# A decoder, cross attention and mixture-of-experts kernel: the cross attention written anew, with all groups in one written-out order over several groups in flight

## What is computed

```
x = layernorm(x + decoder(x))            # 4 layers of causal attention and MLP, and a final norm
x = layernorm(x + xattn(x, ctx_768))
x = layernorm(x + experts(x))            # 8 experts, top 2 of them weighted

def xattn(x, y):                         # y: 120 context rows per sequence
    q = (x @ Wq + bq).reshape(B, N, 16, 16); k, v = likewise from y
    attn = softmax(einsum('bnhd,bmhd->bhnm', q, k) / sqrt(16))
    out  = einsum('bhnm,bmhd->bnhd', attn, v).reshape(B, N, 256)
    return relu(out @ W1 + b1) @ W2 + b2
```

## Time and profile before

| | us |
|---|---|
| median of 3 runs (3950.48 to 3954.08) | 3953.2 |
| the profiled execution itself | 3950.34 |
| its span | 3948.5 |

### The profile page before, as it was taken

The page is one execution under the profiler, slowest core; times in us unless marked ns, Lnnn a source line. Parts: engine busy times, 40 slices in busy tenths (PEclk is TensorE's granted clock), DMA queues, the critical chain, the costliest instruction groups (busy, mean ns, idle before and its releaser), DMA issues. The chain is left out here.

```text
span 3948.5 us, 98572 instructions
## 1 busy us (share of the span) xinstructions
PE 3497.6 (89%) x37088; PEld 2401.6 (61%) x37088; DVE 2361.2 (60%) x4859; ACT 1892.8 (48%) x2713; POOL 1415.3 (36%) x1324
## 2 busy tenths in 40 slices
PE   5899999999999999999955667679999999999998
PEld 3566666666666676666633444446666666666666
DVE  5777777777767777777436676444444434434356
ACT  4666676666766667766623333332222322223222
POOL 1243233332333323333323222134444444444443
PEclk8999999999999999999977778789999999999999
DMA  3100111001110011100011111020000000000000
GB/s 110 45 24 29 45 33 45 27 26 45 33 45 27 26 45 33 45 27 26 18 49 38 44 37 33 23 113 11 11 22 0 22 0 22 20 2 11 0 12 32
DMA packets 103895, 124.22 MB, mean 31 GB/s; under 512 B 17664, under 2 KB 94208, under 8 KB 101120
## 3 DMA queue, kind: packets, MB, share of 16 engines
q1 hardware_dynamic: 103520, 118.78, 9.1%
HBM read 50.13 MB, written 8.39 MB: 15 GB/s over the span
## 5 line engine op out<-in xcount | busy, mean ns | idle before, releaser
L2088 POOL TENSOR_TENSOR e_hT<-e_h,e_hT 128x512 f16<-128x512 f32 x512 | 591.1, 1156 | 775.4 <-DVE e_hT L2054 775.4
L75 PE MATMUL bank<-e_half,e_hT 128*128 128x256 f16 x6144 | 713.7, 273 | 2.6 <-POOL e_hT L2088 2.5
L991 DVE TENSOR_REDUCE mx<-maxima_pair 128x4 f16<-128x1024 f32 (+1 forms) x384 | 470.2, 1224 | 376.8 <-PE maxima_pair L482 374.9
L75 PEld LDWEIGHTS bank<-e_half,e_hT 128*128 128x128 f16 x6144 | 601.8, 98 | 127.2 <-issue 3.3
L2054 DVE CAST e_hT<-e_h 128x512 f16<-128x512 f32 x512 | 301.2, 591 | 448.0 <-ACT e_h L2012 447.8
L75 PE MATMUL bank<-xT,w_half 128*128 128x512 f16 x2304 | 535.4, 383 | 29.4 <-ACT mrow L770 18.3
L1091 POOL TENSOR_TENSOR QK<-qk,QK 128x512 f16<-128x512 f32 x128 | 148.1, 1157 | 1026.3 <-ACT QK L721 985.9
L789 ACT ACTIVATE PR<-scores_pair 128x1024 f32<-128x1024 f32 x384 | 393.0, 1024 | 177.5 <-PE scores_pair L499 97.2
L2012 ACT ACTIVATE e_h<-scores_pair,e_b 128x512 f32<-128x512 f32 x256 | 175.9, 687 | 495.1 <-PE scores_pair L75 449.0
L1098 POOL TENSOR_TENSOR hT<-h,hT 128x512 f16<-128x512 f32 x256 | 291.9, 1168 | 296.8 <-ACT hT L776 296.8
L2012 ACT ACTIVATE e_h<-maxima_pair,e_b 128x512 f32<-128x512 f32 x256 | 175.7, 687 | 456.8 <-PE maxima_pair L75 445.1
(11 more groups left out here) (162 smaller groups left out, 5676.1 us busy)
## 6 DMA issues: line engine op xcount, KB each, us to landing
QS<-QK SPq DMA_DIRECT2D x240, 128.0 KB, 2.1
KS<-QK SPq DMA_DIRECT2D x192, 128.0 KB, 2.1
e_raw<-in_expert_weights SPq DMA_DIRECT2D x16, 1024.0 KB, 5.1
w_raw<-in_weights SPq DMA_DIRECT2D x48, 256.0 KB, 3.1
c_x<-in_x SPq DMA_DIRECT2D x8, 512.0 KB, 4.2
xT_halves<-c_xT SPq DMA_DIRECT2D x16, 256.0 KB, 2.6
out<-e_z SPq DMA_DIRECT2D x8, 512.0 KB, 2.9
x<-in_x SPq DMA_DIRECT2D x1, 3584.0 KB, 15.3
```

What stands on the lines that cost most here:

```text
L75: last = pe.matmul(out, stat(a, k), mov(b, k), start=(k == 0 and n == 0), stop=(k == tiles - 1 and n == 2))
L991: dve.tensor_reduce(out, src, AX.X, ALU.max, negate=True).then_inc(mx_in.sem, 1)
L2088: pool.tensor_tensor(low, h32[:, m % 2, :], hT[odd][0][:, m, :], ALU.subtract)\
```

## The change

`cross` no longer has loops or kinds of bodies. Every engine walks over `BODIES`, and in each body does, in a hand-set order, pieces of up to seven groups. What changes besides the order:

- One joint root for three norms: the first norm of group n, the sum's norm of group n-1 and the last norm of group n-5. Its steps are on 128x12, with twelve aggregations.
- ScalarE makes the high halves of Q, K and of the hidden tiles by a second activation from PSUM; VectorE's two kinds of casts are gone. `h32` has four parts instead of two.
- GpSimd takes over the addition of b2 (`add_bias`, 128x1024) and the low half of the context (`context_low`, 128x480).
- The last norm writes into x, and ScalarE's copy into x is gone. The context halves and the rows of VS for the values are doubled.
- The split of the weights comes ahead of the first sum's norm.

In the diff the first `hidden_high` is VectorE's, the new functions behind it are ScalarE's and GpSimd's, and the last part is the second half of VectorE's body.

```diff
+    BODIES = range(-4, NG + 3)
+    NORMS, LAG = 3, 5
...
-    norm_buf = [NormBuffers(sb, f"c_norm{i}", shared["dve_gate"]) for i in range(3)]
...
+        def joint_root(n):
+            for i, g in enumerate((n, n - 1, n - LAG)):
+                if has(g):
+                    dve.wait_ge(stats_in[i].sem, stats_in[i].after(g))
+                    part_from_wait(dve, shared["dve_gate"])
+            for t in range(NORMS * TT):
+                dve.bn_aggr(mean_var[:, t, :], stats[:, t, :]).then_inc(rooted.sem, 1)
...
-        def hidden_high(n):
-                dve.tensor_copy(hT[0][:, m, :], h32[:, m % 2, :]).then_inc(h_h.sem, 1)
+        def hidden_high(n, m):
+            act.wait_ge(H_ps.sem, H_ps.after(n, m + 1))
+            act.activation(hT[0][:, m, :], work("H", n, m)[:, :], ACT.Relu,
+                           bias=cols[:, 4 + m:5 + m], scale=1.0 / WS).then_inc(h_h.sem, 1)
...
+        def query_key_high(n, m):
+            query_key(n, m, QK[0], qk_h)
...
+        def add_bias(n):
+            pool.wait_ge(z1.sem, z1.after(n))
+            pool.tensor_tensor(x[:, bass.ds(n * TT, TT), :], z[1][:, :, :], row["b2"].unsqueeze(1)
+                               .to_broadcast([P, TT, D]), ALU.add).then_inc(z1b.sem, 1)
...
-        body(PRE, -1, True, False, False)
-        body(HEAD, 0, True, True, False)
-        with eng.Fori(1, NG - 1) as n:
-            body(STEADY, n, True, True, True)
+        for n in BODIES:
...
+            if has(n):
+                maxima(n, 3, 0)
+            if has(n - 2):
+                last_stats(n - 2)
+            if has(n + 2):
+                sum_stats(n + 2)
+            if has(n):
+                maxima(n, 3, 1)
+            if 0 <= n + 3 < NG + LAG:
+                joint_root(n + 3)
+            if has(n + 2):
+                sum_scaled(n + 2)
+            if has(n - 2):
+                last_scaled(n - 2)
+            if has(n + 1):
+                maxima(n + 1, 0, 0)
+            if has(n - 3):
+                router_weights(n - 3)
```

More of the change, by code:

```diff
@@ L1261, in cross, with work, free_tile @@
+    def work(stage, n, k):
+        return W[AT[stage, n, k] % R]
+    def free_tile(pe, stage, n, k):
+        before = AT[stage, n, k] - R
+        if before >= 0:
+            stage, of, part = TILES[before]
+            for signal, each in READERS[stage]:
+                pe.wait_ge(signal.sem, signal.after(of, (part + 1) * each))
+        return W[before % R]
     block_ctx = ExitStack()
@@ L1294, in halves @@
                 sp.wait_ge(s.sem, s.after(n))
-                part_from_wait(sp, shared["sp_gate"])
-                sp.dma_start(xT_halves[half, :, :, bass.ds(n * GT, GT)], xT[1][half][:, :, :])\
+                sp.dma_start(xT_halves[half, :, :, n * GT:(n + 1) * GT], xT[1][half][:, :, :])\
                   .then_inc(halves_out.sem, 16)
[L1299 to L1306, removed]
-            if ahead:
-                heads(n + 1, 1)
-            if back:
-                halves(n - 1)
         sp.dma_start(rows[:, :], dram["cross_rows"].partition_broadcast(P)).then_inc(s_const, 16)
@@ new lines, in outputs @@
+        def outputs(n, k):
+            bank = free_tile(pe, "Y", n, k)
+            if k == 0:
+                pe.wait_ge(h_h.sem, h_h.after(n))
+                pe.wait_ge(h_l.sem, h_l.after(n))
+            for u in range(2):
+                t = 2 * k + u
+                last = split_matmuls(pe, bank[:, u * D:(u + 1) * D], lambda h, kk: hT[h][:, kk, t * P:(t + 1) * P],
+                                     lambda h, kk: views["f2"][h][:, kk, :], KF2)
+            last.then_inc(Y_ps.sem, 1)
@@ L1554, in out_rows @@
             act.activation(OTs[:, c, :], O[:, :], ACT.Copy).then_inc(o_in.sem, 1)
-        def hidden(kind, n):
-            for m in range(KF2):
-                act.wait_ge(H_ps.sem, H_ps.after(n - 1, m + 1))
-                for s in (h_h, h_l):
-                    act.wait_ge(s.sem, s.after(n - 1, m - 1) if m >= 2 else s.after(n - 2, KF2 - 1 + m))
-                act.activation(h32[:, m % 2, :], work(kind, ("H", m))[:, :], ACT.Relu,
-                               bias=cols[:, 4 + m:5 + m], scale=1.0 / WS).then_inc(h_f.sem, 1)
@@ new lines, in scale_tiles, with first_stats, first_scaled @@
+        def scale_tiles(i, n, src, out, done):
+            rstd = root[NEWTON % 2]
+            dve.wait_ge(rooted.sem, rooted.after(n))
+            for t in range(TT):
+                at = i * TT + t
+                dve.tensor_scalar(out(t), src(t), mean_var[:, at, 0:1], rstd[:, at:at + 1], ALU.subtract, ALU.mult)\
+                   .then_inc(done.sem, 1)
+        def first_stats(n):
+            tile_stats(0, x_tiles(n))
+        def first_scaled(n):
+            dve.wait_ge(z1.sem, z1.after(n - 1))
+            scale_tiles(0, n, x_tiles(n), lambda t: z[0][:, t:t + 1, :], zf)
+            if n == 0:
+                split_weights()
```

881 lines of the change are left out of this document (483 added, 398 removed), and 4 rows, old and new, of the table ORDER.

## The result

The changed kernel takes 3772.76 us in the median of four runs, the kernel before 3952.86: a ratio of 0.9551 [0.9533, 0.957], 180 us less. I had predicted 3784, in a range from 3748 to 3832. The profiled execution took 3773.66 us, its span is 3771.8.

What follows compares the result with a forecast made beforehand. Engines taking turns in a chain were taken to bound the body; reordered, VectorE's 31 + 8 and 2 of waits make 41 us, eight bodies 292, with the ends 169 us saved: 3784, range 3748 to 3832.

Steps and rivals of the forecast that it cites:

- What bounds the kernel before, a chain in turns: Loop of `cross`: a 61.38 us body is a chain through engines taking turns, none full; reordering shrinks it.
- TensorE's work, 33 to 34 a body: TensorE in a body of `cross`: 41.0 us at mean clock 0.81 is 33 at full clock; 34 taken.
- my bound of 33: Lower bound on TensorE's work in a body of `cross`: 33 us with full clock throughout.
- VectorE's work, 31 at rest: VectorE in a body of `cross`: 42.7 us less removed casts, additions, roots and a wait is 30.4, with idle time 31.
- What VectorE and GpSimd cost each other, 5.3 at the root and 3 elsewhere: Body of `cross`: VectorE operations with only SBUF operands stand still until GpSimd's end; 8 us more, VectorE at 39.
- a sign: Profile after, full body: small root steps at 0.4 us or more in the mean, VectorE busy over nine tenths.
- The body, 39 + 2: Full body of `cross`: VectorE's 39 us and 2 for waits in order, together 41.
- the 2 us of order: Full body: TensorE's waits for QK's low halves by DMA and of T2 for the last scaling, 2 us.
- Body by body: Bodies 0 to 7 of `cross`, shorter where groups run out: sum 292 us.
- The ends: Around the bodies: first score about 2070, body 0 from 2074, last `attend` ended 2368, 3 us added behind; 169 us saved.
- The first, TensorE as the bound at 3750: Rival: GpSimd's operations meet waits VectorE has anyway, VectorE stays at 33, bodies 35 to 36 us, about 3750; chance 0.18.
- The others: VectorE and GpSimd taking turns throughout, about 3850, 0.18; slower from instruction supply, 3984, 0.03; body stays 61 us, 0.01.

Runs made afterwards that it cites:

- e1: The kernel before with the loops of the cross attention written out, old order and work; 3957.0 us, ratio 1.0014.
- e2: The kernel before with the high halves of Q, K and H made by ScalarE from PSUM instead of VectorE's casts; 3930.2 us, ratio 0.9949.
- e3: The changed kernel with three roots on 128x4, one behind the other, in place of the joint root; 3851.8 us, ratio 0.9754.
- e11: The changed kernel with the high halves of Q, K and the hidden rows cast by VectorE again, not made by ScalarE; 3802.1 us, ratio 0.9623.
- e4: The changed kernel with GpSimd's b2 addition moved behind the first operation of `add_first`, away from VectorE's joint root; 3746.2 us, ratio 0.9480.
- e7: The changed kernel with one key projection of each group computed five times, just ahead of TensorE's wait; 3763.6 us, ratio 0.9530.
- e5: The changed kernel with TensorE's turns of the last norm's rows and their row scores moved behind key scores and half of Y; 3781.3 us, ratio 0.9578.
- e6: The changed kernel with both GpSimd's b2 addition early and TensorE's turns of the last norm's rows later; 3776.0 us, ratio 0.9563.
- e9: The changed kernel with VectorE's two sets of scalings behind the joint root swapped, those of x first; 3776.4 us, ratio 0.9558.

## Why the prediction held, step by step

- **What bounds the kernel before, a chain in turns.** Right. e1 and e2 change neither order nor roots, and stay at bodies of 58 to 63 us. With the new order and three roots (e3) the kernel is already 99 us under its runs of the kernel before (3951.1); of these, going by e11, some 29 are the high halves. The joint root brings the other 79. The 70 that are left I put down to the order, and in part to what went from VectorE to GpSimd; no run has the new order alone.
- **TensorE's work, 33 to 34 a body.** Right for the changed kernel (33.3). But it holds 1.5 us of lower clock: at the clock 1.00 it is 31.8 (e4), below my bound of 33. I had multiplied 41.0 by 0.81, but that is the mean clock of the whole window, TensorE's waits included, and in these it was mostly high. In windows of 1 us, weighted by TensorE's busy time, the clock of the same body is 0.77, and 41.0 x 0.77 = 31.5, near the 31.8 of e4. The fp32 `attend` takes 1.07 at full clock (I had taken 1.28 or less from the earlier trace rows).
- **VectorE's work, 31 at rest.** Too high: it is busy 34.7 with 5.7 us of meetings, so 29.0 without, where the items gave 30.4 and idle time between small steps the rest. Of these 1.4 us, 1.0 are the router's scalings (L1740 before, L1863 after): four of them took 1.4 us before, with a mean of 427 ns, and 0.4 after, 169 each. Before, they met GpSimd's addition to the values, and I had left them in at that price. The last 0.4 stay open.
- **What VectorE and GpSimd cost each other, 5.3 at the root and 3 elsewhere.** The mechanism and the place were right, the size was not: b2 addition and low halves stand beside the root, and cost 3.9 us in its steps and 1.8 in the scalings, together 5.7 instead of 8. The low halves of QK 0 and 1, 1.8 us of the 5.3, run beside the aggregations, which don't stand still. The twelve narrow steps have a mean of 0.49 us (2.22, 1.08, 1.08 and nine of 0.17 or less), as I had named it for a sign; VectorE is busy 91% of the body, where I wanted over nine tenths. That the steps end with GpSimd's operations is what the Trainium skill's page SBUF — State Buffer, section SBUF: two separate sides, says of an exclusive lock, and the trace agrees. e4 shows that it is the meeting and not the work: the same operation at another place gives 27 us back.
- **The body, 39 + 2.** 38.0, 3 less. The sum was that of two errors, and in part luck: VectorE's busy time is 4.3 lower than forecast, and what it does not work 1.4 higher, 3.4 of 38.0 (1.1 for Y, 1.0 for GpSimd, 0.2 for row scores, the rest between its steps). Who is bound is told better from TensorE's side, 33.3 + 4.1 and small waits. I had the wait of T2 for the last scaling among the 2 us of order; it is the largest wait of the body.
- **Body by body.** 31, 35, 39, 41, 41, 40, 34, 31 against 31.2, 26.9, 36.5, 38.0, 38.0, 38.0, 38.9, 32.8; the sum 280 against 292. Body 1 is the largest miss: with 23.7 us of TensorE's work it is that short. Body 6 went the other way. I took 7 us off it since two norms have run out, but the joint root is as wide as ever, GpSimd's bias addition and low halves are still there, TensorE waits the same 4.1, and its clock is lower (0.91).
- **The ends.** First row scores at 2070.83 (forecast 2070), 43.2 us from the last `attend` to the experts (43.4). Between them errors cancel: counted from root to root the bodies begin 6.5 us before the forecast's 2074 and are 12 shorter in sum, but behind them the last `attend` ends 12.2 us later, not 2. From 2580.79 to 2402.97 it is 177.8, where the steps gave 169; the median fell by 180.
- **Rivals.** The first, TensorE as the bound at 3750, was 23 us off where the forecast was 11, and came nearly true in e4, at 3746, with one operation moved: TensorE works 31.8 of 33.5 us there and waits 0.8 for the burst. The others did not come near.

## What to carry over

- When engines work in order, find the stretch of one engine whose end another waits for, and count whose operations it meets in this stretch. Here the wait followed it one for one (17.3, 11.9 and 8.6 us gave waits of 9.6, 4.1 and 0.8). Moving a foreign operation out of it was worth 27 us, swapping operations inside it nothing; moving the waiter made a wait of its own, so that it stays untested (e5, e6).
- Before moving an operation in a written order, look at what else it holds: which bank of the ring it gets next (e5), and what stands right behind it (e9).
- A step that several items share saves in every place where nothing hides it, the ends included: three norms in one root saved 5.3 us in a full body, and 79 over all 13 roots.

## What was not expected of the hardware

- A wait cost more here than its length, by the clock. Behind the wait of 4.1 us that ends at 2174.00 TensorE's 24 matmuls of half of Y took 3.86 us, with a granted clock of 0.56 in the 2 us from 2176.5; behind 1.3 (e7) and 0.8 us (e4) it stayed at 1.00 and they took 2.79. In the next body the clock is low sooner: there the eight turns ahead of them take 1.62 us instead of 1.06, and the 24 take 3.40. In both, TensorE's busy time is 1.5 us above that of e4. Filling the wait with 2.46 us of needless matmuls made the kernel 9 us faster.
- Not every VectorE operation on SBUF stands still beside GpSimd. Four statistics (fp32, 128x256) took 1.40 us in all, both beside an addition of 2.35 us and beside GpSimd's subtractions. The twelve aggregations at 2162.00, too, took 0.90 us beside a subtraction, as they do elsewhere.

```profile
2195.25 1.40 DVE L1717 BATCH_NORM_STATS2 c_stats<-x 128x6 f32<-128x256 f32 x4
2197.64 1.40 DVE L1717 BATCH_NORM_STATS2 c_stats<-c_z 128x6 f32<-128x256 f32 x4 [1.00 <-POOL c_z L1940]
```

```profile
2195.26 2.35 POOL L1940 TENSOR_TENSOR c_z<-c_z,c_x 128x1024 f32<-128x1024 f32 x1
```

The prediction had said it of all operations with only SBUF operands. The same section of the Trainium skill is narrower: it gives the lock to VectorE's operations in a two-port mode or with two SBUF inputs. These statistics have one input, and the trace agrees. But several TENSOR_SCALAR steps with one input stood still (L1733, L1736), and no row here shows which mode an operation runs in. Shown standing still are TENSOR_SCALAR, TENSOR_TENSOR, SCALAR_TENSOR_TENSOR (L1744 at 2349.44, 1.12 us instead of 0.17) and the casts, the scalings with 128x256 as well as steps of twelve columns.
